# Second attention layer: scores from stacked f16 parts, value products in f32, masks gone

## The reference

```python
q = q_tokens @ Wq.T          # layernorm(x) [8,256,128]
k = kv_tokens @ Wk.T         # ctx [8,256,96]
v = kv_tokens @ Wv.T
# split into HEADS=16 heads of DK=8 features
attn = jnp.einsum('bhqd,bhkd->bhqk', q, k) * (1 / sqrt(8))
attn = jax.nn.softmax(attn, axis=-1)
out = jnp.einsum('bhqk,bhkd->bhqd', attn, v)
return out.transpose(...).reshape(8, 256, 128) @ Wo.T
```

## Time and profile before

| | us |
|---|---|
| median of 3 runs | 1686.76 (1685.93 to 1686.81) |
| profiled execution | 1684.98, span 1683.2 |
| before the second layer's attention (to 577.5) | 577.5, TensorE busy 516.1, granted clock .98 |
| its first batch (to 640.8) | 63.3, busy 49.7, clock .89 |
| batches 2 to 5 (to 775.2) | 134.4, busy 121.9, clock .96 |
| batches 6 to 8 (to 875.6) | 100.4, busy 84.0, clock .91 |
| the rest | 807.6, busy 630.0, clock .89 |

### The profile page before, as it was taken

How to read it: one execution, slowest core, us unless ns; L and a number is a source line. 1 busy time by engine, 2 the same in 40 slices (tenths; PEclk the granted TensorE clock), 3 DMA queues, 4 the chain that set the end, 5 groups by cost and what they waited for, 6 DMA issues and landing times. The chain is left out here.

```text
span 1683.2 us, 38856 instructions
## 1 busy us (share of the span) xinstructions
PE 1401.7 (83%) x12529; PEld 1083.9 (64%) x12529; DVE 1133.7 (67%) x3284; ACT 833.0 (49%) x1838; POOL 396.2 (24%) x738
## 2 busy tenths in 40 slices
PE   3899999978999979998966864488868899898977
PEld 2677777765666658777754644366646677677665
DVE  4788888876766668888865454443357877788851
ACT  1666666654333346666642242322246665656633
POOL 2000000011111223433322324643311222222221
PEclk9999999988999989999978877699988999999989
DMA  8999100000000210000001100131110000000000
GB/s 228 279 98 132 0 0 0 0 1 1 1 1 0 68 49 5 3 3 6 4 4 43 35 27 17 41 102 43 35 52 1 2 0 0 0 0 0 1 1 25
DMA packets 109759, 55.06 MB, mean 33 GB/s; under 512 B 44593, under 2 KB 102578, under 8 KB 109474
## 3 DMA queue, kind: packets, MB, share of 16 engines
q1 hardware_dynamic: 106146, 46.53, 15.0%
q0 software_dynamic: 3520, 7.31, 1.3%
HBM read 27.09 MB, written 26.74 MB: 32 GB/s over the span
## 5 line engine op out<-in xcount | busy, mean ns | idle before, releaser
L1491 ACT ACTIVATE Pm<-bank,negm 128x256 f32<-128x256 f32 x528 | 220.8, 470 | 220.3 <-DVE negm L2445 122.6
L1667 PE MATMUL bank<-kT,Qz 64*128 64x256 f32 (+2 forms) x1568 | 309.6, 414 | 16.5 <-DVE negm L2436 4.7
L1671 PE MATMUL bank<-ident,Pm 128*128 128x128 f32 x1568 | 238.0, 288 | 63.6 <-DVE PTs L2456 58.3
L2456 DVE TENSOR_TENSOR PTs<-bank,PTs 128x512 f16<-128x512 f32 x384 | 251.4, 682 | 39.7 <-ACT PTs L1445 38.9
L1671 PEld LDWEIGHTS bank<-ident,Pm 128*128 128x128 f32 x1568 | 181.1, 146 | 140.9 <-issue 95.3
L1667 PEld LDWEIGHTS bank<-kT,Qz 64*128 64x128 f32 (+1 forms) x1568 | 189.7, 194 | 99.2 <-issue 57.4
L1445 ACT ACTIVATE PTs<-bank 128x512 f16<-128x512 f32 (+1 forms) x388 | 215.5, 590 | 3.8 <-PE bank L1671 3.7
L1667 PEld LDWEIGHTS bank<-VxF,PTs 128*128 128x128 f16 (+1 forms) x4672 | 183.3, 100 | 11.6 <-DVE PTs L2456 3.2
L1667 PE MATMUL bank<-VxF,PTs 128*128 128x65 f16 (+3 forms) x4672 | 187.4, 189 | 2.1 <-DVE PTs L2456 1.9
L1491 ACT ACTIVATE Pm<-Pm,negm 128x256 f32<-128x256 f32 x256 | 109.7, 497 | 117.2 <-DVE negm L2436 90.0
L2445 DVE TENSOR_REDUCE negm<-bank 128x2 f32<-128x512 f32 x136 | 93.5, 688 | 47.5 <-PE bank L1667 44.2
(11 more groups left out here) (331 smaller groups left out, 2160.5 us busy)
## 6 DMA issues: line engine op xcount, KB each, us to landing
token_rows_by_expert<-trash SPq DMA_DIRECT2D x10, 1782.0 KB, 18.6
Qz<-token_rows_by_expert SPq DMA_DIRECT2D x62, 66.0 KB, 1.8
R<-expert_rows_by_token SPq DMA_DIRECT2D x12, 256.0 KB, 4.6
R<-in_L_ffn_ew SPq DMA_DIRECT2D x2, 1024.0 KB, 7.3
R<-in_L_ffn_w SPq DMA_DIRECT2D x1, 2048.0 KB, 9.5
R<-in_L_xattn_Wkv SPq DMA_DIRECT2D x2, 768.0 KB, 6.4
R<-in_L_ffn_w SPq DMA_DIRECT2D x1, 1408.0 KB, 12.2
R<-in_L_xattn_Wq SPq DMA_DIRECT2D x2, 512.0 KB, 3.9
```

The lines of the kernel that those rows point to most:

```text
L1491: last = act.activation(masked, masked if A.mask == "full" else bank[k % 2][:, qt * S:(qt + 1) * S], ACT.Exp, bias=negm[:, k % 4, qt:qt + ...
L1667: return pe.matmul(o, l, r, start=start, stop=stop)
L1671: return pe.transpose(o, i, ident[0:n, 0:n])
L2456: dve.tensor_tensor(PTl[:, k % 4, :], bank[2 + k % 2][:, :], PTh[:, k % 4, :], ALU.subtract).then_inc(s.pt[1].sem, 1)
```

## The change

Scores. Queries and keys are split into f16 high and low parts, scaled by factors worked out from the weights' largest entries (`head_scales`), written to DRAM (`head_rows_written`) and read back so that each head has 24 rows: keys high, high, low against queries high, low, high (`in_bands`). Four heads share the 128 partitions. A head's scores are two f16 products of 24 rows by 256 keys. The scale goes into the softmax: VectorE multiplies the maxima by it, ScalarE takes it as the exponentials' scale.

Values. The copy of the turned probabilities is f32, on ScalarE for even heads and on VectorE for odd ones; the subtraction is gone, and av is four f32 products with whole f32 values.

Masks on GpSimd are gone. Queries 0 to 2 move into the last chunk of the feed-forward (`NEXT_QUERIES`), which is written out on TensorE, ScalarE and VectorE; TensorE's six middle batches are written out too. Behind head 1's scores in the first batch stand five f32 products whose result nothing uses (`FILLERS`). The feed-forward's hidden tile `G` moves from `Qz` to a part of `R0`, since `Qz` now takes the queries' bands.

The diff, cut to what the prediction speaks of:

```diff
+FILLERS = 5
...
-    if A.dh != 64:
+    if A.n == 1:
+        return [(kind, j) for kind in "kv" for j in range(4)] + [("q", j) for j in range(3)]
+    if A.n == 2:
         return [(kind, j) for kind in "kv" for j in range(4)]
     return [("k", 0), ("k", 1)] + ([] if A.null else [("k", 2)]) + [("v", 0), ("vlow", 0), ("v", 2), ("vlow", 2)]
...
+NEXT_QUERIES = {(3, 0): ("q", 0), (4, 0): ("q", 1), (5, 0): ("q", 2)}
...
+        G = {0: cols(R0, 0, 2048).rearrange("p (g s) -> p g s", s=CH),
+             3: Qz[:, :, :].rearrange("p h s -> p (h s)").rearrange("p (g s) -> p g s", s=CH)}
+        headscale = sb("headscale", [P, 3])
+        rowmax = sb("rowmax", [P, 4, 2])
+        bandsq = Qz[:, :, :].rearrange("p h s -> p (h s)").bitcast(F16).rearrange("p (j t) -> p j t", t=T)
+        bandsk = [t.bitcast(F16).rearrange("p (j t) -> p j t", t=T)
+                  for t in (kT[:, :, :].rearrange("p h s -> p (h s)"), cols(R0, 9472, 2048))]
+        head_rows = {w: nc.dram_tensor(f"head_rows_{w}", (P, 2, T), F16, kind="Internal").ap() for w in "kq"}
...
+            if A.n == 1 and eng is nc.tensor:
+                for b in range(1, B - 1):
+                    body(b, "mid")
...
+            def head_rows_written(kind, c):
+                s = att_s[1]
+                m = c if kind == "k" else 8 + c
+                if m % 2:
+                    need(sp, s.ring.dve, (m + 1) // 2)
+                else:
+                    need(sp, s.headlow, (c + 4 * (kind == "q")) // 2 + 1)
+                sp.dma_start(head_rows[kind][:, :, c * CH:(c + 1) * CH], head_parts(kind, c)).then_inc(head_rows_out[kind], 16)
+            def in_bands(dst, kind, js, ts, done):
+                src = head_rows[kind].rearrange("(j g d) u t -> u g d j t", j=4, g=4, d=8)
+                for g in range(4):
+                    for i, u in enumerate((0, 0, 1) if kind == "k" else (0, 1, 0)):
+                        sp.dma_start(dst[32 * g + 8 * i:32 * g + 8 * i + 8, :, ts], src[u][g][:, js, ts]).then_inc(done, 16)
+            for c in range(NCH):
+                head_rows_written("k", c)
+            sp.wait_ge(head_rows_out["k"], 16 * NCH)
+            in_bands(bandsk[0], "k", slice(0, 2), slice(0, T), key_bands[0])
+            for c in range(3):
+                head_rows_written("q", c)
+                sp.wait_ge(head_rows_out["q"], 16 * (c + 1))
+                in_bands(bandsq, "q", slice(0, 4), slice(c * CH, (c + 1) * CH), query_bands[0])
             need(sp, ffn_s[0].y, NCH * FFN[0].E)
+            in_bands(bandsk[1], "k", slice(2, 4), slice(0, T), key_bands[1])
...
+            head_rows_written("q", 3)
+            sp.wait_ge(head_rows_out["q"], 16 * 4)
+            in_bands(bandsq, "q", slice(0, 4), slice(3 * CH, T), query_bands[1])
...
-                def masks(b, bw, heads=range(0, 16, 4)):
-                    for h in heads:
-                        if b is not None:
-                            need(pool, s.scores, b * 16 + (h + 4))
-                        plain(pool)
-                        pool.tensor_tensor(
-                            Qz[:, h:h + 4, :], xnT[:, bass.ts(bw, S)].unsqueeze(1).to_broadcast([P, 4, S]),
-                            headmask[:, h:h + 4].unsqueeze(2).to_broadcast([P, 4, S]), ALU.mult).then_inc(s.qm.sem, 1)
...
+                            factor = headscale[:, 2:3] if A.n == 1 else -1.0 if A.mask == "full" else 1.0
                             for qt in range(2):
                                 masked = Pm[:, k % 4, qt * S:(qt + 1) * S]
                                 last = act.activation(masked,
                                                       masked if A.mask == "full" else bank[k % 2][:, qt * S:(qt + 1) * S],
                                                       ACT.Exp, bias=negm[:, k % 4, qt:qt + 1],
-                                                      scale=-1.0 if A.mask == "full" else 1.0)
+                                                      scale=factor)
...
+                        elif kind == "turn" and A.n == 1 and k % 2 == 0:
+                            need(act, s.turn, b * nh + (k + 1))
+                            need(act, s.av, b * nh + (k - 3))
+                            move(PTs[:, k % 4, :], bank[2][:, :]).then_inc(s.pt[0].sem, 1)
+                        elif kind == ("high" if A.dh == 64 else "turn") and A.n != 1 and (A.n != 2 or k % 2 == 0):
                             need(act, s.turn, b * nh + (k + 1))
                             need(act, s.av, b * nh + (k - 3))
                             move((PTs if A.n == 2 else PTh)[:, k % 4, :],
                                  bank[2 + k % 2][:, :]).then_inc(s.pt[0].sem, 1)
-                        elif kind == "v" and A.n != 2 and (m % 2 or A.dh == 64):
+                        elif kind in ("q", "k") and A.n == 1:
+                            i = k + 4 * (kind == "q")
+                            act.wait_ge(head_scale_set, 1)
+                            need(act, s.ring.filled, m + 1)
+                            w = 0 if kind == "q" else 1
+                            move(head_parts(kind, k)[:, 0, :], bank_of(m)[:, :], headscale[:, w:w + 1]).then_inc(s.headhigh.sem, 1)
+                            if m % 2 == 0:
+                                need(act, s.headlow, i // 2 + 1)
+                                act.sem_inc(s.ring.act.sem, 1)
...
-                            if A.n == 1 and k % 4 == 0:
-                                need(pe, s.qm, b * 4 + (k // 4 + 1))
+                            if A.n == 1 and kinds == "first" and k in (0, 8):
+                                pe.wait_ge(key_bands[k // 8], 16 * 12)
+                                if k == 0:
+                                    pe.wait_ge(query_bands[0], 16 * 36)
+                            if A.n == 1 and kinds == "mid" and b == 1 and k == 0:
+                                pe.wait_ge(query_bands[1], 16 * 12)
                             need(pe, s.exp, b * nh + (k - 1))
                             for qt in range(2):
                                 o = bank[k % 2][:, qt * S:(qt + 1) * S]
-                                last = mm(o, Qz[:, k, qt * P:(qt + 1) * P], keys_of(A, b, k))
+                                if A.n == 1:
+                                    rows, j = slice(32 * (k % 4), 32 * (k % 4) + 24), k // 4
+                                    last = mm(o, bandsq[rows, j, b * S + qt * P:b * S + (qt + 1) * P],
+                                              bandsk[j // 2][rows, j % 2, b * S:(b + 1) * S])
+                                else:
+                                    last = mm(o, Qz[:, k, qt * P:(qt + 1) * P], kT[:, k, :])
                             last.then_inc(s.scores.sem, 1)
+                            if A.n == 1 and kinds == "first" and k == 1:
+                                for c in range(FILLERS):
+                                    mm(bank[2][:, :], ident[:, :], xnT[:, bass.ts(c % NCH, CH)])
...
+                            elif A.n == 1:
+                                need(pe, s.pt[k % 2], b * (nh // 2) + (k // 2 + 1))
+                                p = k // 2
+                                if k % 2 == 0:
+                                    need(pe, s.norm, b * 8 + (p - 1))
+                                for qt in range(2):
+                                    r = (k % 2) * 2 + qt
+                                    for kt in range(2):
+                                        last = mm(bank[4 + p % 2][:, r * P:r * P + 9],
+                                                  PTs[:, k % 4, kt * S + qt * P:kt * S + (qt + 1) * P],
+                                                  Vhead(A, b if k >= 0 else b - 1, kt, k % 16, VxF), kt == 0, kt == 1)
...
+            def head_scales(A):
+                q, k, both = (headscale[:, i:i + 1] for i in range(3))
+                dve.tensor_scalar(q, vmaxall[:, 4:5], P / 2.0 ** 13, 2.0 ** -60, ALU.mult, ALU.max)
+                link(dve.tensor_scalar(k, vmaxall[:, 5:6], vmaxall[:, 0:1], DC / 2.0 ** 13, ALU.mult, ALU.mult))
+                link(dve.tensor_scalar(k, k, 2.0 ** -60, None, ALU.max))
+                link(dve.tensor_scalar(both, k, q, A.scale, ALU.mult, ALU.mult))
+                dve.reciprocal(headscale[:, 0:2], headscale[:, 0:2]).then_inc(head_scale_set, 1)
...
+                                chain(dve.tensor_reduce(rowmax[:, k % 4, :], v, AX.X, ALU.max, negate=True))
+                                dve.tensor_scalar(nm, rowmax[:, k % 4, :], headscale[:, 2:3], None,
+                                                  ALU.mult).then_inc(s.negmax.sem, 1)
...
-                            need(dve, s.pt[0], b * nh + (k + 1))
-                            dve.tensor_tensor(PTl[:, k % 4, :], bank[2 + k % 2][:, :], PTh[:, k % 4, :],
-                                              ALU.subtract).then_inc(s.pt[1].sem, 1)
+                            if A.dh == 64:
+                                need(dve, s.pt[0], b * nh + (k + 1))
```

(41 more changed lines are left out.)

96 lines of the change are left out of this document (44 added, 52 removed).

## The result

The changed kernel takes 1814.78 us (median of 4 runs, 1810.50 to 1817.88) against 1686.78 before: a ratio of 1.0757, 95% interval 1.0733 to 1.0781. It is 128 us slower, far outside the range of 1650 to 1685. The profiled execution is 1810.50 us with a span of 1808.8.

The account below looks back on a forecast made before the run. The prediction took TensorE to set the pace, 3.40 us for two heads. Its terms summed to -16.8 us on the profiled 1684.98, 1668.2, or 1670 against the median of 1686.76; the range was 1650 to 1685.

Parts of the forecast that it names:

- The clock: Second layer's attention: granted clock .95 or more from 640 to 860, since f32 transposes ran at 1.00 in the earlier trace.
- R1: Rival, chance .13: loop gaps of .3 per pair drop TensorE to 1.2 GHz; 6.3 per pair, 1729 for a third of pairs.
- The sum: Whole kernel: -7.3 to the first addition, -6.1 for four batches, -3.4 for the rest; -16.8 us together.
- one clock term: Low clock behind the tiny 128x8 operation's stall late in a batch: 1.5 us on the path, gone after the change.
- Scores: Each head: two f16 products replace four f32 records of .95; .21 plus .1 for the narrow tile, ends 0 and .3.
- the loop of 3.57 through VectorE: Two heads, from VectorE to TensorE and back: ends last at 3.57 us, .17 over 3.40, +1.4 per batch.
- choose stall: Late in 7 of 8 batches: the 128x8 VectorE operation takes 1.89 beside a GpSimd mask; 1.72 saved each.
- R2: Rival, chance .20: choosing experts still makes TensorE wait in each batch and the clock fall behind it; +10.5, 1680.
- The start: First heads of the second layer's attention: third scores start at 586.0 instead of 585.04, +1.0 us.
- R3: Rival, chance .13: nine-column value products cost half, 3.1 us per pair; 1650.
- R4: Rival, chance .06: the all-reduce of block maxima still makes VectorE wait before head 15; +10.9, 1681.
- R5: Rival, chance .04: the fourth q's bands come late for the second batch, up to 10 us; 1680.

Follow-up runs that it names:

- the bursts: Changed kernel plus unused work ahead of head 8's transposes in every second-layer batch: 24 f32 products of 128x128, 1841.6 us, or 48 f32 transposes, 1841.5 us.
- the version with 128 columns: Changed kernel with value products of up to 128 columns instead of 9, the others never read: 1665.11 us, ratio .9876 to the kernel before.
- the one with 128 rows: Changed kernel with each score product on all 128 rows instead of 24, so the scores are other numbers than the layer's: 1778.9 us.

## Why the prediction was wrong, step by step

**The clock** is the step that failed. The sum took every part of the new head at the 2.4 GHz level and put nothing in for the loss of that level; it left it to a rival, R1, at a chance of .13. The runs showed in its place that TensorE is at 1.2 GHz from head 7 of the first batch on: a head takes 3.09 instead of the 1.62 worked out, a batch 52.45 instead of 32.1.

R1 named the mechanism, and its price per pair was right (6.3, measured 2 x 3.09 = 6.18). What it had wrong is how long and why. It laid the fall to gaps of .3 in TensorE and spoke of a third of the pairs. The first fall did come at waits, but the bursts show that the level is lost without any gap, and it stays lost for about 60 of 64 pairs.

I read from the earlier trace rows that transposes go with a full clock, which is right, and let that stand for the new head, in which the f32 scores, .95 of 1.71 us, are replaced by .32 of scores and .89 of nine-column products. By the experiments it is the going of the f32 scores that lost the level. The text itself said that no row shows such a mix; an unknown that decides the sign should have had a far larger chance.

The Trainium skill's sentence on transposes (TensorE: Matmul & The Clock Gate, Part 4), against which I argued, is not what failed here: in the burst of 48 transposes the granted clock went to 1.00, so this trace disagrees with it again.

**The sum** can be read in the version with 128 columns, in which the clock holds and all but that width is as in the change. VectorE's additions of its timed run:

```profile
630.47 0.42 DVE L2635 TENSOR_TENSOR xnew<-bank,x 128x256 f32<-128x256 f32 x1 [0.18 <-PE bank L1715]
...
762.44 0.42 DVE L2635 TENSOR_TENSOR xnew<-bank,x 128x256 f32<-128x256 f32 x1 [0.18 <-PE bank L1715]
...
853.34 0.42 DVE L2635 TENSOR_TENSOR xnew<-bank,x 128x256 f32<-128x256 f32 x1 [1.80 <-PE bank L1715]
```

To the first addition -10.3 (predicted -7.3), the four batches behind it -2.4 (-6.1), the rest to the last -9.6 (-3.4): together -22.3 against -16.8, and 1665.1 against my 1670. That this is so near is partly luck: no stretch came nearer than 3 us, and -3.0, +3.7 and -6.2 partly cancel. Of the last, one part is plain: the last batch took 30.00 at a clock of .83 before (845.64 to 875.64) and takes 25.15 at 1.00 here (828.19 to 853.34), and the prediction left out one clock term there. One by one:

- Scores take .32, as I took (.21 and .1). But the narrow scores also lengthen their neighbours, also at the high level. Rows of the changed kernel, then of the one with 128 rows:

```profile
587.64 0.96 PE L1715 MATMUL bank<-VxF,PTs 128*128 128x9 f32 x8
588.46 0.64 PE L1719 MATMUL bank<-ident,yn 128*128 128x128 f32 x4
...
584.23 0.39 PE L1715 MATMUL bank<-kT,Qz 128*128 128x256 f16 x2 [0.45 <-ACT Pm L1526]
584.46 0.60 PE L1719 MATMUL bank<-ident,Pm 128*128 128x128 f32 x4
```

  Scores to transposes .32 against .23 on all rows, transposes .49 against .43, value products .89 ahead of narrow scores against .82. Together some .23 per head, where the sum has .1 and its upper end .3: this term was mis-sized. The Trainium skill says that a change of tiling mode drains TensorE (TensorEngine Tiling (Array Packing), Key Properties). The trace agrees so far that each of the three stretches beside a change is longer; that a drain is the reason, no run here shows.
- Value products of 9 columns .82 to .89, where .88 was taken.
- TensorE's own work for two heads is 2 x 1.70 = 3.40 in the changed kernel at the high level and 2 x 1.80 = 3.60 with 128 columns; 3.24 was predicted. So in the version with 128 columns TensorE sets the pace in most pairs, not the loop of 3.57 through VectorE, which nothing here measures by itself. Two of its heads, without a gap:

```profile
657.37 0.39 PE L1715 MATMUL bank<-kT,Qz 24*128 24x256 f16 x2
...
660.97 0.39 PE L1715 MATMUL bank<-kT,Qz 24*128 24x256 f16 x2
```

- VectorE's reductions are 3.66 apart in the pair below and 3.60 in others; the multiplication behind each takes .23, not .17.

```profile
617.30 0.69 DVE L2527 TENSOR_REDUCE rowmax<-bank 128x2 f32<-128x512 f32 x1 [0.17 <-PE bank L1715]
618.03 0.23 DVE L2528 TENSOR_SCALAR negm<-rowmax,headscale 128x2 f32<-128x2 f32 x1
...
619.17 0.68 DVE L2527 TENSOR_REDUCE rowmax<-bank 128x2 f32<-128x512 f32 x1
...
620.96 0.69 DVE L2527 TENSOR_REDUCE rowmax<-bank 128x2 f32<-128x512 f32 x1 [0.20 <-PE bank L1715]
```

- A batch is 33.0, not 32.1. Eight pairs of 3.60 are 28.8 of it; and TensorE still waits for VectorE's copies, 14.7 us in all from 645 to 840, 2.5 per batch, where VectorE's operations between the heads were put at nothing.
- The choose stall of the earlier trace rows is gone: the operation on 128x8 takes .16 in all eight batches. TensorE still waits for VectorE behind the choice of experts, .41 and .88 us in the batch at 645, but the clock stays at 1.00 from 640 to 840. So of R2 a part of the wait is there, and its price is not.

```profile
679.47 0.16 DVE L2734 TENSOR_TENSOR rk<-ohacc 128x8 f32<-128x8 bf16 x1
```

- The start: the third scores come 4.92 us behind the start of the fillers, in the changed kernel (579.09 and 584.01) and in the version with 128 columns (580.41 and 585.33); 5.4 was predicted, from 580.6 to 586.0. The fillers end ahead of them.
- R3 is out (.82 to .89), R4 is out (no wait at head 15), R5 did not show.

What stays open: why a head with the new scores and nine-column value products loses the level, and one with f32 scores or with 128 columns keeps it, is known here only as a list of mixes. Of the nine-column head the bursts show that it can't keep the level. Of the other mixes at .50 it is shown that they fell among the first heads, where TensorE also waits, and did not lift the clock again; whether they would keep it without those waits was not tried.

## What to carry to other kernels

A change that makes TensorE's products smaller has to be priced at both levels of its clock, and the level isn't decided by busy time: read the clock row beside the busy row. If a group of products takes hardly longer with more columns, as eight records of 128 (.89 to .99) against eight of 9 (.82 to .89) here, columns that nobody reads cost little and can keep the clock; try that before giving a change up. And if the one unknown in a sum can turn its sign, it belongs in the chances with its own weight, not behind the sum.

## What the runs showed of the hardware

- TensorE at 100% busy ran at .50 for 390 us, and lost 1.00 again behind each burst with no gap between its instructions; at 75% busy it kept 1.00 from 590 to 600 in the version with 128 columns.
- 48 f32 transposes in a row lift the granted clock from .50 to 1.00 as 24 f32 products do.
- Eight f32 records with 128-column weights take, ahead of scores on 24 rows, .89 with 9 columns and .99 with 128 at 2.4 GHz, and 1.65 with 9 at 1.2 GHz; ahead of a product on all rows .82, .89 and 1.57.
- Score products on 24 of 128 rows take .32 us to the next start at the high level, those on all rows .23; at the low one .54 and .38. With their neighbours they cost some .23 more per head at the high level and .28 at the low one.
